# The product with gamma of four of five groups on GpSimd in the first experts' combining

## The chip, the cores and the metric

The kernel runs on one core of one Trainium2 chip. The metric is the device time of one execution in microseconds (us), lower being better. Several engines work side by side: TensorE (PE in the profile, its weight loads PEld), VectorE (DVE), ScalarE (ACT), GpSimd (POOL) and SyncE (SP, which issues transfers). Each engine runs its own instructions in order, and engines wait for one another through semaphores.

## The reference, cut to what matters

The program computes two rounds, each a graph stage followed by a mixture of experts. The change lies at the end of the first experts (16 experts, two for each row, rows of 256 values). For each of the 3125 rows:

```python
moe = jnp.sum(topk_w[..., None] * sel, axis=2)     # two weighted results of experts
y = x + moe                                        # here x is the normalised row, xn in the kernel
mu = jnp.mean(y, axis=-1, keepdims=True)
var = jnp.var(y, axis=-1, keepdims=True)
return (y - mu) / jnp.sqrt(var + EPS) * gamma + beta
...
x = x + _L0_ffn_ref(_layernorm(x, axis=-1)[None], ...)[0]
x = x + _L1_gnn_ref(_layernorm(x, axis=-1), ...)   # the next stage wants the normalised new x
```

## The kernel before

Rows lie on 128 partitions in 25 tiles of 256 values (`NT`); five tiles make a group (`J = 5`), so there are five groups (`NJ = 5`), and an operation on one group is 128 x 1280 values.

`feed_forward` runs the experts. Its last results are written by GpSimd to a buffer in memory (`put_rows`, line 2376), and then the class `Finish` combines them. SyncE reads both results of all rows back (`Finish.sync`, lines 2492 and 2495, into the tiles `f_hits` and `h`), and VectorE and ScalarE work through the five groups in turn. In the trace the rows being combined (`y`) are called `f_hits`, the running x is `parts_and_x`, and gamma is `f_gamma`.

On VectorE (`Finish.vector`) there are these steps for a group i:

- `sum_up(i)`: ten operations that add the two weighted results to xn (line 2553, five for each result), then the moments of the rows (lines 2538 to 2546: five collections of statistics and seven small operations).
- `scale_first(i)`: waits for ScalarE's square root of the variance (line 2509), then a reciprocal and a product of 128 x 5 (lines 2568 and 2569).
- `join(i)`: waits until ScalarE has normalised the group, multiplies by gamma (line 2560) and adds to x (line 2561). beta was added to x earlier.
- moments of the new x (lines 2538 to 2546 again, on `parts_and_x`).
- `scale_next(i)`: waits for the square root of that variance (line 2517), then five small operations (lines 2577 to 2584).

The steps of several groups are interleaved, and the order is written out by hand:

```python
for i in range(NJ):
    sum_up(i)
    if i:
        if i >= 2:
            scale_next(i - 2)
        join(i - 1)
    scale_first(i)
    if i:
        moments(c.x, 1, i - 1).then_inc(self.s_var2, 1)
scale_next(NJ - 2)
join(NJ - 1)
```

ScalarE (`Finish.scalar`) runs `normalise(0)`, and then `normalise(i)` and `next_rows(i - 1)` for each further group. `normalise(i)` is the square root of line 2509 and, after `scale_first(i)`, five operations that normalise the group's tiles (line 2513). `next_rows(i)` is the square root of line 2517 and, after `scale_next(i)`, five operations that make the rows for the next stage (line 2524). So the five operations of `next_rows(i - 2)` stand ahead of the square root of `normalise(i)` on ScalarE. SyncE stores each finished group (line 2499). GpSimd has nothing in this stretch after its last `put_rows`.

When the last group is stored, all engines meet, and the next stage starts: the aggregation over the edges, with its first operations in lines 701 to 809.

Of the kernel before, what the change touches and what calls it, by code (L numbers as in the profile page):

```python
# [7 lines left out]
ALU = mybir.AluOpType  # L8
# [11 lines left out]
P = 128  # L20
N, E, D = 3125, 103125, 256
# [4 lines left out]
J = 5  # L26
NJ = NT // J
# [63 lines left out]
class Steps:  # L91


    def __init__(self, engine, sem):
        self.engine, self.sem, self.base, self.n = engine, sem, 0, 0
# [85 lines left out]
def bc(ap, shape):  # L181
    return ap.to_broadcast(shape)
# [1781 lines left out]
def feed_forward(nc, c, I, name, ne, nf, tiles, softmax_first, logits, w1, b1, w2, b2, norm, act_fn, weight, slot, xn_table, ys, h_table, out):  # L1964
# [9 lines left out]
    with Core(nc) as k:  # L1974
# [61 lines left out]
        finish = None  # L2036
        if out is None:
            got = [hits_room[:, 0:NT * D].rearrange("p (t d) -> p t d", d=D), c.h[:, :, :]]
            finish = Finish(nc, c, k, name, I, ys, weight, got, b2s[:, :, :].rearrange("p e d -> p (e d)"), h_table)
        with nc.Block() as block:  # L2040
# [321 lines left out]
            @block.gpsimd  # L2362
            def _(pool):
                def add_rows(t):
                    pool.wait_ge(s_yb, t + 1)
                    if t:

                        pool.wait_ge(s_added[(t - 1) % Y], 16 * ((t - 1) // Y + 1))
                    pool.sem_inc(s_ask, 1)
                    pool.indirect_dma_start(ys, bass.IndirectOffsetOnAxis(ap=home[:, t:t + 1], axis=0), yb[:, t % Y, :], None, compute_op=ALU.add)\  # L2370
                        .then_inc(s_added[t % Y], 16)

                def put_rows(t):
                    pool.wait_ge(s_yb, t + 3)
                    pool.sem_inc(s_ask, 1)
                    pool.indirect_dma_start(ys, bass.IndirectOffsetOnAxis(ap=home[:, t:t + 1], axis=0), yb[:, t % Y, :], None).then_inc(s_added[t % Y], 16)

                Core.clear(pool)
                pool.wait_ge(s_token, 1)
                if out is not None:  # L2380
                    pool.wait_ge(s_home, 1)
                    pool.wait_ge(s_start, 32)
                else:
                    finish.clear_rest(pool)
                for t in range(tiles):
                    if t >= Q:

                        pool.wait_ge(s_xt, t - Q + 2)
                    pool.sem_inc(s_ask, 1)
                    pool.indirect_dma_start(xb[:, t % Q, :], None, xn_table,  # L2390
                                            bass.IndirectOffsetOnAxis(ap=token[:, t:t + 1], axis=0)).then_inc(s_x[t % Q], 16)
                    if out is not None and t >= Q:
                        add_rows(t - Q)
                    if out is None and t >= Q:
                        if t == Q:
                            pool.wait_ge(s_home, 1)
                        put_rows(t - Q)
                for t in range(tiles - Q, tiles):
                    if out is not None:
                        add_rows(t)  # L2400
                    else:
                        put_rows(t)


class RowNorm:
# [34 lines left out]
class Finish:  # L2440
# [3 lines left out]
    def __init__(self, nc, c, k, name, I, ys, weight, got, out_room, h_table):  # L2444
        self.nc, self.c, self.I, self.ys, self.weight, self.got, self.h_table = nc, c, I, ys, weight, got, h_table
        self.gamma, self.beta = k.sb(f"{name}_gamma", [P, D]), k.sb(f"{name}_beta", [P, D])
        self.out = out_room[:, 0:2 * J * W1].rearrange("p (q j d) -> p q j d", q=2, j=J)
        self.clip = k.sb(f"{name}_clip", [P, 2, NT])
        self.stats = k.sb(f"{name}_stats", [P, 2, J, 6])
        self.mean, self.gap, self.var, self.root = (k.sb(f"{name}_{x}", [P, 2, J]) for x in ("mean", "gap", "var", "root"))  # L2450
        self.rstd, self.down, self.rstd_src, self.down_src = (k.sb(f"{name}_{x}", [P, J]) for x in ("rstd", "down", "rstd_src", "down_src"))
        self.s_got = [k.sem(f"{name}_got{i}") for i in range(NJ)]
        self.s_saved = [k.sem(f"{name}_saved{q}") for q in range(2)]
        (self.s_gb, self.s_rest, self.s_clip, self.s_degrees, self.s_shift,  self.s_var1, self.s_root1, self.s_down1,
         self.s_even, self.s_var2, self.s_root2, self.s_down2, self.s_row, self.s_last) = (
            k.sem(f"{name}_n{x}") for x in ("gb", "rest", "clip", "degrees", "shift",  "var1", "root1", "down1",
                                            "even", "var2", "root2", "down2", "row", "last"))

    def tiles_of(self, i):
        return slice(i * J, i * J + J)  # L2460
# [5 lines left out]
    def clear_rest(self, pool):  # L2466
        for rows in self.got:
            pool.memset(rows[:, NT - 1, :], 0.0).then_inc(self.s_rest, 1)

    def degrees(self, act):  # L2470
        act.wait_ge(self.s_clip, 1)
# [61 lines left out]
    def vector(self, dve, v, st):  # L2533
        c, y, stats, mean, gap, var = self.c, self.got[0], self.stats, self.mean, self.gap, self.var

        def moments(rows, q, i):
            for j in range(J):
                last = v.bn_stats(stats[:, q, j, :], rows[:, i * J + j, :])
            st.link(last)
            v.tensor_tensor(mean[:, q, :], stats[:, q, :, 1], stats[:, q, :, 4], ALU.add)  # L2540
            v.tensor_tensor(gap[:, q, :], stats[:, q, :, 1], stats[:, q, :, 4], ALU.subtract)
            st.link(v.tensor_tensor(var[:, q, :], stats[:, q, :, 2], stats[:, q, :, 5], ALU.add))
            v.tensor_scalar_mul(mean[:, q, :], mean[:, q, :], -0.5)
            v.tensor_tensor(gap[:, q, :], gap[:, q, :], gap[:, q, :], ALU.mult)
            st.link(v.tensor_scalar(var[:, q, :], var[:, q, :], 1.0 / D, EPS, ALU.mult, ALU.add))
            return v.scalar_tensor_tensor(var[:, q, :], gap[:, q, :], 0.25, var[:, q, :], ALU.mult, ALU.add)

        def sum_up(i):
            dve.wait_ge(self.s_got[i], 32 if i < NJ - 1 else 64)
            for q in range(2):  # L2550
                for t in range(i * J, i * J + J):
                    to = c.xn[:, t, :] if q == 0 else y[:, t, :]
                    last = v.scalar_tensor_tensor(y[:, t, :], self.got[q][:, t, :], self.weight[:, q, t:t + 1], to, ALU.mult, ALU.add)
                st.link(last)
            moments(y, 0, i).then_inc(self.s_var1, 1)

        def join(i):
            ts = self.tiles_of(i)
            dve.wait_ge(self.s_even, (i + 1) * J)
            st.link(v.tensor_tensor(y[:, ts, :], y[:, ts, :], bc(self.gamma[:, :].unsqueeze(1), [P, J, D]), ALU.mult))  # L2560
            st.link(v.tensor_tensor(c.x[:, ts, :], c.x[:, ts, :], y[:, ts, :], ALU.add))

        def scale_first(i):
            dve.wait_ge(self.s_root1, i + 1)
            if i:

                dve.wait_ge(self.s_even, i * J)
            st.link(v.reciprocal(self.rstd[:, :], self.root[:, 0, :]))
            v.tensor_tensor(self.down[:, :], mean[:, 0, :], self.rstd[:, :], ALU.mult).then_inc(self.s_down1, 1)

        def scale_next(i):
            ts = self.tiles_of(i)
            dve.wait_ge(self.s_root2, i + 1)
            if i:

                dve.wait_ge(self.s_row, i * J)
            st.link(v.reciprocal(c.h_rstd[:, ts], self.root[:, 1, :]))
            st.link(v.tensor_tensor(c.h_down[:, ts], mean[:, 1, :], c.h_rstd[:, ts], ALU.mult))
            v.tensor_tensor(self.rstd_src[:, :], c.h_rstd[:, ts], c.norm_src[:, ts], ALU.mult)
            v.tensor_tensor(self.down_src[:, :], c.h_down[:, ts], c.norm_src[:, ts], ALU.mult).then_inc(self.s_down2, 1)  # L2580
            if i >= 2:

                dve.wait_ge(self.s_saved[i % 2], 16 * (i // 2))
            v.tensor_copy(self.out[:, i % 2, :, D], c.norm_src[:, ts]).then_inc(self.s_last, 1)

        dve.wait_ge(self.s_shift, NT)
        v.memset(self.out[:, :, :, D:W1], 0.0)
# [11 lines that stand above are left out]
        moments(c.x, 1, NJ - 1).then_inc(self.s_var2, 1)  # L2599
        scale_next(NJ - 1)  # L2600
# [241 lines left out]
```

## Time and profile before

| what | value |
|---|---|
| median of 3 runs | 3093.87 us (3089.11 to 3099.95) |
| the profiled execution, its own time | 3092.59 us |
| its span, from the first to the last instruction | 3091.0 us |
| TensorE busy | 2442.2 us (79%) |
| VectorE busy | 1786.1 us (58%) |
| GpSimd busy | 1742.3 us (56%) |
| ScalarE busy | 1450.7 us (47%) |

The span is the time between the first and the last instruction, and 1.6 us of the execution's own time lie around it. Shares of busy time are averages over stages that have different limits; the stretch that the change touches is about 80 us long, from 1361 to 1444 us after the span's start, and is read by itself.

### The profile page before, as it was taken

To read this page: it belongs to the slowest core of one execution; us is meant where nothing else is said; L and a number is where in the kernel's file an instruction comes from. 1 tells how busy PE (TensorE), PEld (TensorE's weight loads), DVE (VectorE), ACT (ScalarE), POOL (GpSimd) and SP (SyncE) were. 2 spreads that over 40 slices of the span, in tenths; PEclk is the share of its full clock that TensorE was granted. 3 is DMA by queue.
4 is the path that set the end of the run, shared out by engine and by line. 5 is a ranking of instruction groups with operands and counts; after the bars stand their busy time and mean duration, and the time that the engine had idled before them with its cause. 6 is when DMAs were issued, how large, how long until landed. Compare 5 with 4: busy or idle time off the path is not lost. (4 is left out here: it accounts for less than half of the span.)

```text
span 3091.0 us, 52879 instructions
## 1 busy us (share of the span) xinstructions
PE 2442.2 (79%) x14195; PEld 1910.2 (62%) x14195; DVE 1786.1 (58%) x5132; ACT 1450.7 (47%) x3766; POOL 1742.3 (56%) x1702
## 2 busy tenths in 40 slices
PE   1759999969999489850877777787877775899997
PEld 0336666747777478750655555555555554799996
DVE  7669889747788521037776666666666666311110
ACT  0357666535565333333644444444444433455553
POOL 1647777667774045422777777777777750233332
PEclk9989999989999589985998999988898987899998
DMA  6748777578886233543666666666666643443232
GB/s 226 253 143 233 227 209 211 168 227 257 263 251 186 85 109 103 168 128 125 197 186 185 180 186 184 182 182 187 181 187 185 190 119 101 121 106 77 49 65 64
DMA packets 289373, 516.56 MB, mean 167 GB/s; under 512 B 79344, under 2 KB 137057, under 8 KB 287084
## 3 DMA queue, kind: packets, MB, share of 16 engines
q0 software_dynamic: 86192, 225.20, 28.2%
q1 hardware_dynamic: 185532, 267.85, 26.4%
q10 hardware_dynamic: 17392, 20.46, 2.0%
q8 instruction: 116, 1.90, 0.2%
q14 instruction: 141, 1.16, 0.1%
HBM read 381.08 MB, written 137.11 MB: 168 GB/s over the span
## 5 line engine op out<-in xcount | busy, mean ns | idle before, releaser
L726 POOL DMA_INDIRECT agg_r_rows<-h_table,parts_and_x x832 | 831.0, 999 | 336.9 <-issue 230.1
L817 PE MATMUL agg_r_sums<-agg_r_rows,agg_r_onehot 128*128 128x257 f32 x1664 | 489.4, 422 | 259.9 <-DVE agg_r_rows L798 171.8
L817 PEld LDWEIGHTS agg_r_sums<-agg_r_rows,agg_r_onehot 128*128 128x128 f32 x1664 | 305.4, 203 | 396.3 <-issue 318.0
L686 ACT ACTIVATE agg_r_gap<-iota,parts_and_x 128x128 f32<-128x128 f32 x832 | 286.6, 392 | 449.8 <-PE agg_r_sums L817 419.8
L780 DVE TENSOR_TENSOR acc<-acc,agg_r_sums 128x257 f32 (+1 forms) x834 | 351.9, 422 | 129.1 <-PE agg_r_sums L817 44.9
L1723 POOL DMA_INDIRECT rl_buf<-r_table,kinds x304 | 327.6, 1078 | 150.0 <-issue 78.9
L2119 PEld LDWEIGHTS f_pH<-f_xT,f_w 128*128 128x128 f32 x2816 | 332.3, 195 | 40.0 <-ACT f_xT L2197 17.9
L2119 PE MATMUL f_pH<-f_xT,f_w 128*128 128x128 f32 x2816 | 346.7, 280 | 9.9 <-ACT f_xT L2197 4.5
L831 PE MATMUL agg_r_spread<-xn 128*128 128x257 bf16 x2664 | 350.2, 292 | 0.0
L1526 PE MATMUL la_acc<-la_parts,la_counts 128*128 128x512 f32 x1250 | 309.1, 404 | 29.3 <-DVE la_parts L1633 29.3
L2138 PE MATMUL f_pY<-f_w,f_hT 128*128 128x256 f32 x1408 | 325.6, 381 | 7.5 <-DMA f_w<-in_L_ffn_w 7.5
L831 PEld LDWEIGHTS agg_r_spread<-xn 128*128 128x128 bf16 x2664 | 279.6, 105 | 75.7 <-issue 10.0
L2206 ACT ACTIVATE f_hT<-f_pH,f_b 128x128 f32<-128x128 f32 x704 | 197.6, 372 | 263.9 <-PE f_pH L2119 263.6
L1723 POOL DMA_INDIRECT rm_buf<-r_table,kinds x250 | 245.1, 980 | 85.4 <-issue 66.8
L1526 PEld LDWEIGHTS la_acc<-la_parts,la_counts 128*128 128x128 f32 x1250 | 235.0, 190 | 89.9 <-issue 42.2
L2138 PEld LDWEIGHTS f_pY<-f_w,f_hT 128*128 128x128 f32 x1408 | 259.2, 191 | 39.3 <-DMA f_w<-in_L_ffn_w 8.6
L1433 DVE TENSOR_SCALAR b_oh<-b_numbers,b_code 128x400 bf16<-128x400 f16 x980 | 254.7, 324 | 0.0
L798 DVE TENSOR_TENSOR agg_r_rows<-agg_r_rows,agg_r_rel 128x514 f32<-128x514 f32 x305 | 211.0, 692 | 58.2 <-DMA agg_r_rows<-h_table,parts_and_x 56.9
L2370 POOL DMA_INDIRECT f_ys<-f_yb,f_home x56 | 88.2, 1575 | 272.8 <-DVE f_yb L2360 258.9
L1312 PE MATMUL b_strips<-b_oh,b_at 128*128 128x400 bf16 x980 | 199.1, 334 | 50.0 <-DVE b_oh L1433 44.5
L1566 ACT ACTIVATE la_counts<-matrix 128x640 fp32r<-128x640 fp8e4 x250 | 184.0, 737 | 112.8 <-PE la_acc L1526 85.8
L2354 DVE TENSOR_TENSOR f_plain<-f_pY,f_b 128x256 f32<-128x256 f32 x56 | 23.8, 425 | 361.8 <-PE f_pY L2138 361.8
(418 smaller groups left out, 3596.8 us busy)
## 6 DMA issues: line engine op xcount, KB each, us to landing
agg_r_rel<-relation_rows SPq DMA_DIRECT2D x305, 260.0 KB, 3.0
relation_rows<-rl_buf SPq DMA_DIRECT2D x152, 260.0 KB
relation_rows<-rm_buf SPq DMA_DIRECT2D x125, 260.0 KB, 3.3
agg_r_rows<-h_table,parts_and_x POOLq DMA_INDIRECT x832, 3.2
f_w<-in_L_ffn_W SPq DMA_DIRECT2D x18, 512.0 KB, 5.4
f_w<-in_L_ffn_W SPq DMA_DIRECT2D x9, 1024.0 KB, 4.8
f_w<-in_L_ffn_w SPq DMA_DIRECT2D x30, 256.0 KB, 3.1
f_w<-in_L_ffn_w SPq DMA_DIRECT2D x15, 512.0 KB, 3.6
```

Of the source, the lines that this page charges most:

```text
L686: last = nc.scalar.activation(gap[:, n % HOT, t, :], c.iota[:, 0:P], ACT.Abs, bias=c.tab["b_near"][:, column(g) + t:column(g) + t + 1])
L726: pool.indirect_dma_start(rows[:, n % SLOTS, t, :], None, table, bass.IndirectOffsetOnAxis(ap=indices[:, t:t + 1], axis=0)).then_inc(s_row ...
L780: v.tensor_tensor(here, here, sums[:, (2 * (n - LAG) + t) % BANKS, 0:used], ALU.add).then_inc(s_acc, 1)
L798: last = v.tensor_tensor(here, here, rel[:, n % SLOTS, :, 0:used], ALU.mult)
L817: last = nc.tensor.matmul(sums[:, (2 * n + t) % BANKS, 0:used], onehot[:, n % HOT, t, :], rows[:, n % SLOTS, t, 0:used], start=True, stop= ...
L831: last = nc.tensor.matmul(spread[:, t, 0:used], hot[:, r % 2, q, t * P:(t + 1) * P], parts[:, q, part, 0:used], start=q == 0 and part == 0 ...
L1312: last = nc.tensor.matmul(strips[:, n % BANKS, 0:CODES], at[:, n % 2, t, :], oh[:, n % 2, t, :], start=t == 0, stop=t == DEEP - 1)
L1433: last = v.tensor_scalar(oh[:, n % 2, t, :], numbers[:, :], code[:, q, 1, own, t:t + 1], None, ALU.is_equal)
L1526: last = nc.tensor.matmul(acc[:, n % 2, :], counts[:, i, j, :], parts[:, s, :], start=s == 0, stop=s == NT - 1)
L1723: pool.indirect_dma_start(self.buf[:, n, g, :], None, self.table, bass.IndirectOffsetOnAxis(ap=self.c.kinds[:, at:at + 1], axis=0)).then_i ...
L2119: last = nc.tensor.matmul(pH[s][:, f * P:(f + 1) * P], w1b[:, s, f // (FC // 2), at:at + P], xT[:, s, h, :], start=h == 0, stop=h == KD - 1)
L2138: last = nc.tensor.matmul(pY[s][:, 0:D], hT[:, s, f, :], w2b[:, s, f, :], start=f == 0, stop=f == FC - 1)
```

## The change

For the first four groups the product with gamma moves from VectorE to GpSimd. GpSimd makes the four products after its last `put_rows`, each as one instruction on 128 x 1280 values, and each waits until ScalarE has normalised the five tiles of the group (`s_even`). VectorE's addition of those groups waits for a new semaphore, `s_gamma`. The fifth group is as before.

```diff
@@ -2400,6 +2400,9 @@
                         add_rows(t)
                     else:
                         put_rows(t)
+                if finish:
+                    pool.wait_ge(finish.s_gb, 32)
+                    finish.products(pool)
...
@@ -2466,6 +2469,13 @@
...
+    def products(self, pool):
+        y = self.got[0]
+        for i in range(NJ - 1):
+            ts = self.tiles_of(i)
+            pool.wait_ge(self.s_even, (i + 1) * J)
+            self.nc.gpsimd.tensor_tensor(y[:, ts, :], y[:, ts, :], bc(self.gamma[:, :].unsqueeze(1), [P, J, D]), ALU.mult).then_inc(self.s_gamma, 1)
...
@@ -2556,8 +2566,11 @@
         def join(i):
             ts = self.tiles_of(i)
-            dve.wait_ge(self.s_even, (i + 1) * J)
-            st.link(v.tensor_tensor(y[:, ts, :], y[:, ts, :], bc(self.gamma[:, :].unsqueeze(1), [P, J, D]), ALU.mult))
+            if i < NJ - 1:
+                dve.wait_ge(self.s_gamma, i + 1)
+            else:
+                dve.wait_ge(self.s_even, (i + 1) * J)
+                st.link(v.tensor_tensor(y[:, ts, :], y[:, ts, :], bc(self.gamma[:, :].unsqueeze(1), [P, J, D]), ALU.mult))
             st.link(v.tensor_tensor(c.x[:, ts, :], c.x[:, ts, :], y[:, ts, :], ALU.add))
```

On GpSimd, at the end of the first experts and the start of the aggregation (`f_ys` is the experts' buffer, `agg_r_rows` the rows gathered for the aggregation, and `L136` clears semaphores):

```order
 L2376 DMA f_ys<-f_yb,f_home 14592x256 x5
+L2478 TENSOR_TENSOR f_hits<-f_hits,f_gamma 128x1280 x4
 L2040 UNCONDITIONAL_BRANCH
 L719 UNCONDITIONAL_BRANCH
 L726 DMA agg_r_rows<-h_table,parts_and_x 128x260 x24
-L136 ISA x48
+L136 ISA x49
```

Four products stand behind the last write of results and ahead of the end of the stage; one more semaphore is cleared among the aggregation's gathers.

On VectorE, at the combining of the second group, from the end of `scale_next(0)` over `join(1)` to `scale_first(2)`, in the kernel before:

```order
L2580 TENSOR_TENSOR f_down_src<-h_down,norm_src 128x5
L2584 COPY f_b<-norm_src 128x5
L2560 TENSOR_TENSOR f_hits<-f_hits,f_gamma 128x1280
L2561 TENSOR_TENSOR parts_and_x<-parts_and_x,f_hits 128x1280
L2568 RECIPROCAL f_rstd<-f_root 128x5
L2569 TENSOR_TENSOR f_down<-f_mean,f_rstd 128x5
```

The same place in the changed kernel:

```order
L2593 TENSOR_TENSOR f_down_src<-h_down,norm_src 128x5
L2597 COPY f_b<-norm_src 128x5
L2574 TENSOR_TENSOR parts_and_x<-parts_and_x,f_hits 128x1280
L2581 RECIPROCAL f_rstd<-f_root 128x5
L2582 TENSOR_TENSOR f_down<-f_mean,f_rstd 128x5
```

One large operation is gone between `scale_next` and `scale_first`, and the addition stands alone there; at the first, third and fourth group it is the same.

## Rows read from the trace of the kernel before

**Rows 1.** Busy us by stretch: length, PE, PEld, DVE, ACT, POOL, clock, DMA.

```profile
1370.00:1437.80 67.80, 0.00 (x0) 0.00 (x0) 64.62 (x215) 24.86 (x56) 0.00 (x0) 0.50 0.34 111
```

**Rows 2.** Timeline, GpSimd: start us, length us, operation, [idle before].

```profile
1445.59 0.99 POOL L726 DMA_INDIRECT agg_r_rows<-h_table,parts_and_x  x1 [83.57 <-PE agg_r_sums L809]
```

**Rows 3.** Timeline, end of the stretch: the last rows, the next stage's first work.

```profile
1437.68 2.56 ACT L2524 ACTIVATE f_b<-parts_and_x,f_down_src,f_rstd_src 128x256 f32<-128x256 f32 x5 [0.73 <-DVE f_down_src L2580]
...
1444.16 0.59 PE L809 MATMUL agg_r_sums<-zero_b 128*128 128x257 bf16 x2 [84.49 <-PEq L2040]
```

**Rows 4.** Timeline, VectorE and ScalarE at the first group's combining.

```profile
1376.93 0.21 ACT L2509 ACTIVATE f_root<-f_var 128x5 f32<-128x5 f32 x1 [19.43 <-DVE f_var L2546]
...
1377.17 0.19 DVE L2568 RECIPROCAL f_rstd<-f_root 128x5 f32<-128x5 f32 x1 [0.27 <-ACT f_root L2509]
...
1377.60 2.56 ACT L2513 ACTIVATE f_hits<-f_hits,f_down,f_rstd 128x256 f32<-128x256 f32 x5 [0.46 <-DVE f_down L2569]
...
1379.57 2.07 DVE L2553 SCALAR_TENSOR_TENSOR f_hits<-h,f_weight,f_hits 128x256 f32<-128x256 f32 x5
1381.68 1.73 DVE L2538 BATCH_NORM_STATS2 f_stats<-f_hits 128x6 f32<-128x256 f32 x5
1383.44 0.17 DVE L2540 TENSOR_TENSOR f_mean<-f_stats 128x5 f32<-128x5 f32 x1
...
1384.23 1.48 DVE L2560 TENSOR_TENSOR f_hits<-f_hits,f_gamma 128x1280 f32<-128x1280 f32 x1
1384.35 0.21 ACT L2509 ACTIVATE f_root<-f_var 128x5 f32<-128x5 f32 x1 [4.19 <-DVE f_var L2546]
1385.75 1.49 DVE L2561 TENSOR_TENSOR parts_and_x<-parts_and_x,f_hits 128x1280 f32<-128x1280 f32 x1
```

**Rows 5.** Timeline, VectorE and ScalarE at the second group's combining.

```profile
1387.70 2.56 ACT L2513 ACTIVATE f_hits<-f_hits,f_down,f_rstd 128x256 f32<-128x256 f32 x5 [3.14 <-DVE f_down L2569]
...
1390.13 2.06 DVE L2553 SCALAR_TENSOR_TENSOR f_hits<-f_hits,f_weight,xn 128x256 f32<-128x256 f32 x5
...
1397.53 1.48 DVE L2560 TENSOR_TENSOR f_hits<-f_hits,f_gamma 128x1280 f32<-128x1280 f32 x1
1397.58 2.57 ACT L2524 ACTIVATE f_b<-parts_and_x,f_down_src,f_rstd_src 128x256 f32<-128x256 f32 x5 [7.12 <-DVE f_down_src L2580]
1399.05 1.49 DVE L2561 TENSOR_TENSOR parts_and_x<-parts_and_x,f_hits 128x1280 f32<-128x1280 f32 x1
1400.05 0.19 ACT L2509 ACTIVATE f_root<-f_var 128x5 f32<-128x5 f32 x1
...
1400.57 0.19 DVE L2568 RECIPROCAL f_rstd<-f_root 128x5 f32<-128x5 f32 x1
```

**Rows 6.** GpSimd's groups by shape, first 5 us: busy us, mean ns | idle before.

```profile
L426 POOL IOTA matrix<- 128x808 int32 x1 | 0.8, 801 | 0.0
L420 POOL IOTA wide_i<- 128x512 int32 x1 | 0.6, 554 | 0.7 <-POOLq L201 0.7
L211 POOL TENSOR_SCALAR_AFFINE_SELECT ident<-ident 128x128 f32<-128x128 f32 x1 | 0.3, 282 | 0.0
...
L424 POOL TENSOR_SCALAR_AFFINE_SELECT alive<-alive 128x1 f32<-128x1 f32 x1 | 0.2, 186 | 0.1
```

**Rows 7.** Timeline, GpSimd issuing gathers beside trains of VectorE, two places.

```profile
84.76 7.88 DVE L1073 TENSOR_SCALAR parts_and_x<-parts_and_x,ln_mean,ln_var 128x256 f32<-128x256 f32 x24
...
85.72 6.83 POOL L1723 DMA_INDIRECT r_buf<-r_table,kinds  x1 [0.30 <-issue]
...
850.61 4.29 DVE L1633 TENSOR_TENSOR la_parts<-parts_and_x,la_parts 128x1280 fp32r<-128x1280 f32 x3
...
850.72 2.19 POOL L1723 DMA_INDIRECT rm_buf<-r_table,kinds  x1 [0.30 <-issue]
```

**Rows 8.** By source line, count, min/median/max ns: VectorE products, GpSimd gathers.

```profile
L1633 DVE TENSOR_TENSOR la_parts<-parts_and_x,la_parts x12: 418/1484/1493, 656.2 to 864.0; 128x1280 fp32r<-128x1280 f32 x8, 128x1024 fp32r<-128x1024 f32 x2, 128x256 fp32r<-128x256 f32 x2
...
L726 POOL DMA_INDIRECT agg_r_rows<-h_table,parts_and_x x832: 949/953/1662, 1445.6 to 2528.9; - x167
```

More of the change, by code:

```diff
@@ L2454, in __init__ @@
         (self.s_gb, self.s_rest, self.s_clip, self.s_degrees, self.s_shift,  self.s_var1, self.s_root1, self.s_down1,
-         self.s_even, self.s_var2, self.s_root2, self.s_down2, self.s_row, self.s_last) = (
+         self.s_even, self.s_var2, self.s_root2, self.s_down2, self.s_row, self.s_last, self.s_gamma) = (
             k.sem(f"{name}_n{x}") for x in ("gb", "rest", "clip", "degrees", "shift",  "var1", "root1", "down1",
-                                            "even", "var2", "root2", "down2", "row", "last"))
+                                            "even", "var2", "root2", "down2", "row", "last", "gamma"))
     def tiles_of(self, i):
```

## The prediction

> **What bounds the kernel now.** The change touches one stretch, the combining at the end of the first experts, so the shares over the whole span say little. I read the busy time by stretch first. From 1370.0 to 1437.8 us VectorE is busy for 64.62 of 67.80 us, ScalarE for 24.86, GpSimd and TensorE not at all [rows 1]. VectorE is the bound there. The timeline says the same: its operations stand end to end, and ScalarE mostly waits for it. The last rows are made at 1437.68, and the next stage's first matmul stands at 1444.16 with nothing beside this work [rows 3], so time taken from VectorE's chain should shorten the whole execution by as much, as long as nothing else is late next. GpSimd's next work in the trace is the gather at 1445.59, after 83.57 us of idle time [rows 2]; the products find it free, and no transfer of GpSimd's own stands behind them before the stage ends. The one more semaphore to clear, among the aggregation's gathers, I cost at nothing: gathers follow each other there without a gap that the clearing of the other 48 makes.
>
> **What is removed from VectorE.** A product with gamma takes 1.48 us, and the addition behind it starts 1385.75 - 1384.23 = 1.52 us after it [rows 4]. Four go: 6.08 us of VectorE's work. That is not yet time gained; what is late next has to be looked up at each place.
>
> First group. Without the product the addition stands at 1384.23 and ends at about 1385.7. Behind it is the reciprocal of `scale_first(1)`, which needs ScalarE's square root of 1384.35, done at 1384.56 [rows 4]. It is ready, so the whole 1.52 us is gained.
>
> Second group. The addition moves from 1399.05 to 1397.53 and ends at 1397.53 + 1.49 = 1399.02 [rows 5]. Behind it the reciprocal of `scale_first(2)` needs ScalarE's square root, and on ScalarE that stands behind the five operations of `next_rows(0)`, which VectorE itself released only at 1397.58 and which take 2.57 us. The root runs from 1400.05 to 1400.24 [rows 5]. Where VectorE has had to wait for a root, it went on 0.03 us after its end: 1376.93 + 0.21 against 1377.17 [rows 4]. So the reciprocal comes at 1400.27 instead of 1400.57 [rows 5]: of 1.52 us only 0.30 is gained, and 1.22 us becomes a wait for ScalarE. The third and fourth groups repeat this order. The fifth keeps its product.
>
> Sum of what can be gained: 1.52 + 3 x 0.30 = **2.42 us** of the 6.08.
>
> **What is added on GpSimd.** Each product waits for the end of ScalarE's five normalising operations: 1377.60 + 2.56 = 1380.16 for the first [rows 4], 1387.70 + 2.56 = 1390.26 for the second [rows 5]. The additions want them at 1384.23 and 1397.53. So there is a cover of 4.07 us for the first product and 7.27 us for the later ones. The queue behind a VectorE that waits for a product holds everything that follows: the addition, `scale_first`, and through it ScalarE.
>
> The trace of before has no product on GpSimd, so its price T is bounded. A generation of numbers costs (801 - 554) / (808 - 512) = 0.83 ns an element above some 0.13 us [rows 6]; 1280 elements in one such pass are 1.2 us, the lower end. Two reads and a write, each as a pass of its own, are 3 x 1.07 + 0.13 = 3.3 us, the upper end. The selection that reads 128 elements and writes 128 takes 282 ns against 186 ns for one, 0.76 ns an element [rows 6], so a read and its write go in one pass, and a second operand makes two: T = 2 x 1.07 + 0.13 = 2.3 us, which I take. All three lie under both covers, so VectorE would not wait for the products as such.
>
> In the Trainium skill, "GPSIMD Engine Reference" (section 3.1, Elementwise) has 4497 ns for an addition of two operands of 2048 elements; 1280 elements are then an estimated 2.8 us. No run here shows it yet, and it too lies under the covers.
>
> **What the two engines do to each other.** This decides the sign. The first product becomes ready at 1380.16, within VectorE's train of five operations at 1379.57, each with two inputs in the on-chip memory; behind it are 1.73 us of statistics with one input (from 1381.68), then small operations with two inputs (from 1383.44) [rows 4]. The second becomes ready at 1390.26, just after the train at 1390.13 has begun [rows 5]. Two places show GpSimd beside such trains. Beside 24 one-input operations an issue that takes 0.95 us otherwise [rows 8] took 6.83 us and ended as the train did; beside 128x1280 products with two inputs one took 2.19 us [rows 7], while those products kept to 1484 ns, at most 1493 [rows 8]. In both GpSimd waited and VectorE did not.
>
> So my forecast lets each product wait until the train ends and run from 1381.68 beside the statistics. It ends at 1381.68 + 2.3 = 1383.98, and the small operation of 1383.44 waits 0.54 us for it. With T = 1.2 that wait is zero, with 3.3 it is 1.57 us. Four times 0.54 is 2.16 us (0 to 6.3). Sum: -2.42 + 2.16 = **-0.26 us**, with ends at -2.4 and +3.9.
>
> The profiled execution took 3092.59 us, of which 3091.0 is span; the median of the runs is 3093.87. Against the profiled execution this gives 3092.3 us, against the median 3093.6, and that I forecast; ends 3091.5 and 3097.7.
>
> **Rivals.**
>
> Rival 1, GpSimd holds VectorE off (slower). A product that gets in between two operations of a train stops the train for its whole length. Each of the four costs T, in a part where ScalarE is not what VectorE waits for: 4T - 2.42, which is +2.4 us at 1.2, +6.8 at 2.3 and +10.8 at 3.3. It is slower than before from T = 0.61 us on. For it: the issue at 850.72 took 2.19 us, so it got going at about 852.0, as the first of the products ended and with the next directly behind it [rows 7]; GpSimd found its way in between. Against it: no operation of VectorE in these rows is longer for it, though an issue is not a reading product. Time: 3100.7 us.
>
> The Trainium skill's "SBUF — State Buffer" (section "Who interferes with whom") has this as a rule: a VectorE instruction with two inputs there and a GpSimd instruction that reads there exclude each other, and whichever is second waits until the first is done. Which one is first the page leaves to the order of issue. With the other page's estimate of 2.8 us the rival would cost +8.8 us.
>
> Rival 2, the two engines do not touch. Then all 2.42 us are gained: 3091.5 us. For it: VectorE's times beside issues are flat. Against it: GpSimd's are not [rows 7].
>
> Rival 3, the product is far dearer than its bounds. Above T = 4.07 the first addition waits; above 7.27 + 1.22 = 8.49 the later ones cost as well. At 12 us this is 12 - 4.07 - 1.52 + 3 x (12 - 8.49 - 0.30) = +16.0 us, 3109.9. Against it: no first use of an operation on GpSimd in the rows shows such a price [rows 6].
>
> That the change does nothing is no rival: the order on the engines shows four products on GpSimd and four fewer on VectorE.
>
> **How the numbers follow.** Forecast 0.40, rival 1 0.30, rival 2 0.23, rival 3 0.07. The measurement can tell about 0.3% from no change, 9.3 us here; the bounds are 3084.6 and 3103.2. No case goes below the lower one, since only 2.42 us are to be had: 0.03 for differences between runs. Above the upper one lies rival 1 with T over 2.93 us, about a third of it, and most of rival 3: 0.13. The rest, 0.84, is within. The range runs from 3089.5, which is rival 2 less 2 us for the spread of the median (the three runs span 10.8 us), to 3101.5, which takes in rival 1 up to T = 2.5 us. Outside lie the dearer part of rival 1, rival 3 and a little below, some 2 in 10.
>
> **What would show it.** On VectorE, reciprocals of `scale_first(2)` to `scale_first(4)` that wait about 1.2 us for ScalarE's root, and additions that start without a wait for GpSimd. On GpSimd, four products of 1.2 to 3.3 us that end after the train. If the forecast holds, the operations of the trains keep their 0.42 us and the small operation behind the statistics starts late. If rival 1 holds, one operation of a train has a gap or a length of about T. If rival 2 holds, neither. The stretch from 1370.05 to the last rows would be shorter by 0.3 us, longer by 7, or shorter by 2.4. A difference of more than 12 us from the median, or one that lies outside this stretch, would make the prediction wrong in its kind.

## The result, and the profile after

The changed kernel is slower. Over 20 runs of each, it took 3103.75 us (median; 3095.21 to 3112.26) against 3092.65 us (3086.37 to 3101.50). The ratio is 1.0032 with a 95% interval of 1.0022 to 1.0042, which is 9.9 us, between 6.8 and 13.0 (the medians lie 11.1 us apart). The forecast was 3093.6 us with a range up to 3101.5, so the time lies outside it, on the side of rival 1.

The profiled execution of the changed kernel took 3095.21 us with a span of 3093.6 us. It is the shortest of the 20, so the place of the loss is read from the combining stretch and not from the span. I measure that stretch on VectorE, from the start of the first weighted sum to the start of the last small copy of `scale_next(4)`. Before it is 1370.05 to 1437.57, which is 67.52 us; after it is 1363.91 to 1439.65, which is 75.74 us: **8.22 us longer**. That lies inside the interval of 6.8 to 13.0 us. The first and last operation, before and after:

```profile
1370.05 2.07 DVE L2553 SCALAR_TENSOR_TENSOR f_hits<-f_hits,f_weight,xn 128x256 f32<-128x256 f32 x5 [9.63 <-DMA h<-f_ys]
...
1437.57 0.17 DVE L2584 COPY f_b<-norm_src 128x5 f32<-128x5 f32 x1
```

```profile
1363.91 2.07 DVE L2563 SCALAR_TENSOR_TENSOR f_hits<-f_hits,f_weight,xn 128x256 f32<-128x256 f32 x5 [9.69 <-DMA h<-f_ys]
...
1439.65 0.17 DVE L2597 COPY f_b<-norm_src 128x5 f32<-128x5 f32 x1
...
1439.77 2.56 ACT L2534 ACTIVATE f_b<-parts_and_x,f_down_src,f_rstd_src 128x256 f32<-128x256 f32 x5 [0.73 <-DVE f_down_src L2593]
...
1446.29 0.59 PE L809 MATMUL agg_r_sums<-zero_b 128*128 128x257 bf16 x2 [92.81 <-PEq L2040]
```

From the start of the last rows to the next stage's first matmul it is 1446.29 - 1439.77 = 6.52 us, against 6.48 before [rows 3], so nothing is lost at the border to the next stage.

The busy times of this stretch, the columns as in [rows 1]:

```profile
1363.90:1439.70 75.80, 0.00 (x0) 0.00 (x0) 69.02 (x211) 24.75 (x55) 11.87 (x4) 0.50 0.30 99
```

VectorE has four instructions fewer and is busy for longer (69.02 us against 64.62), and GpSimd is busy for 11.87 us with four products, 2.97 us each. ScalarE is unchanged (the window of before only reaches a little way into its last five operations). An engine that does less work and is busy longer is being held up inside its instructions. VectorE's idle time in these windows grows as well, from 3.18 to 6.78 us; that comes from the wait shown for the second group below, which occurs three times. The timeline at the first group, which answers to [rows 4], shows where:

```profile
1373.44 4.69 DVE L2563 SCALAR_TENSOR_TENSOR f_hits<-h,f_weight,f_hits 128x256 f32<-128x256 f32 x5
1374.18 2.88 POOL L2478 TENSOR_TENSOR f_hits<-f_hits,f_gamma 128x1280 f32<-128x1280 f32 x1 [18.36 <-ACT f_hits L2523]
1378.16 1.73 DVE L2548 BATCH_NORM_STATS2 f_stats<-f_hits 128x6 f32<-128x256 f32 x5
1379.93 0.17 DVE L2550 TENSOR_TENSOR f_mean<-f_stats 128x5 f32<-128x5 f32 x1
...
1380.72 1.48 DVE L2574 TENSOR_TENSOR parts_and_x<-parts_and_x,f_hits 128x1280 f32<-128x1280 f32 x1
```

The train of five operations takes 4.69 us instead of 2.07. The product starts inside it and takes 2.88 us; the statistics and the small operations behind it are as they were. The addition at 1380.72 follows the small operations without a wait, 3.7 us after the product's end, so it is not the new semaphore that costs. By source line (count, min/median/max ns), the two trains before, then the two after, and the one operation by itself in a narrow window:

```profile
L2553 DVE SCALAR_TENSOR_TENSOR f_hits<-f_hits,f_weight,xn x25: 478/480/485, 1370.0 to 1418.3; 128x256 f32<-128x256 f32 x25
L2553 DVE SCALAR_TENSOR_TENSOR f_hits<-h,f_weight,f_hits x25: 476/480/485, 1372.2 to 1420.4; 128x256 f32<-128x256 f32 x25
```

```profile
L2563 DVE SCALAR_TENSOR_TENSOR f_hits<-f_hits,f_weight,xn x25: 470/477/3103, 1363.9 to 1420.7; 128x256 f32<-128x256 f32 x25
L2563 DVE SCALAR_TENSOR_TENSOR f_hits<-h,f_weight,f_hits x25: 472/480/3104, 1366.0 to 1422.7; 128x256 f32<-128x256 f32 x25
```

```profile
1374.23 3.10 DVE L2563 SCALAR_TENSOR_TENSOR f_hits<-h,f_weight,f_hits 128x256 f32<-128x256 f32 x1
```

The medians are those of before (480 ns; operations of a train start 0.40 us apart and overlap, so that five take 2.07 us), the longest are 3.10 us. Each of the four products meets one train, and in it exactly one operation is long: it starts 0.05 us (first group) to 0.18 us after the product does and ends 0.28 us after the product's end. That is one operation held for the length of one product.

The second group, which answers to [rows 5]:

```profile
1385.09 4.68 DVE L2563 SCALAR_TENSOR_TENSOR f_hits<-f_hits,f_weight,xn 128x256 f32<-128x256 f32 x5
...
1385.31 3.00 POOL L2478 TENSOR_TENSOR f_hits<-f_hits,f_gamma 128x1280 f32<-128x1280 f32 x1 [8.25 <-ACT f_hits L2523]
1389.81 2.07 DVE L2563 SCALAR_TENSOR_TENSOR f_hits<-h,f_weight,f_hits 128x256 f32<-128x256 f32 x5
...
1395.12 1.49 DVE L2574 TENSOR_TENSOR parts_and_x<-parts_and_x,f_hits 128x1280 f32<-128x1280 f32 x1
1395.17 2.56 ACT L2534 ACTIVATE f_b<-parts_and_x,f_down_src,f_rstd_src 128x256 f32<-128x256 f32 x5 [9.75 <-DVE f_down_src L2593]
1397.64 0.19 ACT L2519 ACTIVATE f_root<-f_var 128x5 f32<-128x5 f32 x1
...
1397.92 0.19 DVE L2581 RECIPROCAL f_rstd<-f_root 128x5 f32<-128x5 f32 x1 [1.31 <-issue]
```

Here the first train of the next sum is hit, the second is untouched. And the reciprocal of `scale_first(2)` now waits 1.31 us. The profile names no releaser for it, but it starts 0.09 us after the end of ScalarE's root (1397.64 + 0.19). The prediction had this wait, with 0.03 us after the root.

### The profile page after: what moved, and what is told of

It reads as the page before. It is cut to its first block and busy times, and to the rows that moved or that the text cites. A ratio compares the mean times of both kernels' runs of the same rounds, so it can differ in the third digit from the quotient of the medians.

```text
span 3093.6 us, 52881 instructions
## 1 busy us (share of the span) xinstructions
PE 2442.4 (79%) x14195; PEld 1909.0 (62%) x14195; DVE 1789.9 (58%) x5128; ACT 1450.6 (47%) x3766; POOL 1760.7 (57%) x1706
## 5 line engine op out<-in xcount | busy, mean ns | idle before, releaser
L1723 POOL DMA_INDIRECT rm_buf<-r_table,kinds x250 | 244.2, 977 | 85.4 <-issue 70.8
```

The costliest lines, as they stand in the source:

```text
L1723: pool.indirect_dma_start(self.buf[:, n, g, :], None, self.table, bass.IndirectOffsetOnAxis(ap=self.c.kinds[:, at:at + 1], axis=0)).then_i ...
```

## The experiments

Two theories for the held operations. Theory 1: a GpSimd instruction that reads the on-chip memory holds off a VectorE instruction with two inputs there, for its whole length. Theory 2: any work of GpSimd slows VectorE. A third question was whether the rest of the loss comes from elsewhere. All runs at a glance, with the stretch as defined above, the aggregation behind it from its first sum to its last, and the time of the execution that was profiled. Each experiment's stretch comes from one profile:

| run | stretch, us | aggregation, us | execution, us |
|---|---|---|---|
| kernel before, three profiles | 67.52, 67.51, 67.49 | 1090.7, 1095.4, 1096.4 | 3092.59, 3091.01, 3093.56 |
| changed kernel, three profiles | 75.74, 75.73, 75.74 | 1093.2, 1101.1, 1092.7 | 3095.21, 3109.64, 3103.42 |
| products behind the train | 69.60 | 1095.5 | 3097.96 |
| spare product | 78.03 | 1096.3 | 3113.25 |
| spare copy | 71.46 | 1100.3 | 3105.04 |
| spare zeroing | 67.48 | 1092.5 | 3094.73 |
| five small products | 73.24 | 1098.8 | 3102.56 |
| root first | 72.44 | 1095.4 | 3103.99 |
| products behind the train, root first | 66.22 | 1097.1 | 3097.17 |
| three tiles on GpSimd | 64.33 | 1104.4 | 3101.03 |

**Products behind the train.** The product waits in addition for the last operation of VectorE's second train.

```diff
             pool.wait_ge(self.s_even, (i + 1) * J)
+            pool.wait_ge(self.s_link, self.train_end[i + 1])
...
```

Further lines, not shown, note on VectorE where each train ends.

> The changed kernel, but each product on GpSimd also waits until VectorE's train of ten two-input operations (sum_up of the next group) has ended. The combining stretch, from VectorE's first weighted sum to its last small copy, is 67.5 us in the kernel before and 75.7 us in the changed one. Theory 1 (a GpSimd instruction that reads on-chip memory holds off VectorE instructions with two inputs there, for its whole length, and no others): the trains take 2.07 us again, the statistics keep 1.73 us beside the product, and the first small two-input operation behind them waits about 1.4 us; stretch 67.5 - 2.3 + 4 x 1.4 = 70.8 us. Theory 2 (any work on GpSimd slows VectorE): the statistics grow by about 2.6 us as the trains did; stretch 75.7 us.

The timeline:

```profile
1377.10 2.07 DVE L2565 SCALAR_TENSOR_TENSOR f_hits<-h,f_weight,f_hits 128x256 f32<-128x256 f32 x5
1379.20 1.73 DVE L2550 BATCH_NORM_STATS2 f_stats<-f_hits 128x6 f32<-128x256 f32 x5
1379.35 2.88 POOL L2479 TENSOR_TENSOR f_hits<-f_hits,f_gamma 128x1280 f32<-128x1280 f32 x1 [19.82 <-DVE f_hits L2565]
1380.97 1.29 DVE L2552 TENSOR_TENSOR f_mean<-f_stats 128x5 f32<-128x5 f32 x1
1382.18 0.15 DVE L2553 TENSOR_TENSOR f_gap<-f_stats 128x5 f32<-128x5 f32 x1
```

The train is back at 2.07 us. The statistics, one input each, run beside the product in their 1.73 us. The first small operation with two inputs takes 1.29 us instead of 0.17 and ends as the product does. This is what my forecast drew, made by force, and it still makes the stretch 2.1 us longer than before: four waits of 1.1 us against 2.2 us gained. (The 70.8 us that I had expected came of waits of 1.4 us.) Theory 2 is out for the statistics, the only VectorE instructions with one input that ran beside a product here.

**Spare work on GpSimd.** Three kernels keep all products on VectorE and only let GpSimd do something at the same four moments, into a place that nobody reads: a product, a copy, or zeros.

```diff
+            pool.wait_ge(self.s_even, (i + 1) * J)
+            if i:
+                pool.wait_ge(self.s_spare, i)
+            self.nc.gpsimd.tensor_tensor(self.spare, self.got[1][:, ts, :], bc(self.gamma[:, :].unsqueeze(1), [P, J, D]), ALU.mult).then_inc(self.s_spare, 1)
...
```

The others have `tensor_copy(self.spare, self.got[1][:, ts, :])` and `memset(self.spare, 0.0)` in its place.

> The kernel before, with all of its products on VectorE, and beside them four products of 128x1280 on GpSimd at the moments of the changed kernel, read from finished rows and written to a spare place that nobody reads or waits for. Theory 1: one operation of each train is held by 2.6 us; stretch 67.5 + 4 x 2.62 = 78.0 us. Were the loss of the changed kernel a wait for the product's result instead, nothing would wait here: 67.5 us.

> As the spare product, but GpSimd copies 128x1280 values (one input read, one output written). Theory 1: the copy reads on-chip memory, so it holds VectorE's two-input operation for its own length, some 1.2 to 1.5 us: one operation of each train 0.8 to 1.2 us longer, stretch 70.7 to 72.3 us. If only instructions of GpSimd with two inputs hold VectorE off: 67.5 us.

> As the spare product, but GpSimd sets 128x1280 values to zero (nothing read). Theory 1: no operation of VectorE is longer than in the kernel before; stretch 67.5 us. Theory 2: one operation of each train is longer by about the length of the instruction, some 1 us; stretch 71 us.

The first group's operation meets VectorE's second train (`h,f_weight,f_hits`), the other three meet its first (`f_hits,f_weight,xn`). By source line, both trains beside the product:

```profile
L2567 DVE SCALAR_TENSOR_TENSOR f_hits<-f_hits,f_weight,xn x25: 472/477/3124, 1371.6 to 1430.4; 128x256 f32<-128x256 f32 x25
L2567 DVE SCALAR_TENSOR_TENSOR f_hits<-h,f_weight,f_hits x25: 471/479/3127, 1373.7 to 1432.5; 128x256 f32<-128x256 f32 x25
```

Beside the copy, and the copy itself:

```profile
L2567 DVE SCALAR_TENSOR_TENSOR f_hits<-f_hits,f_weight,xn x25: 471/479/1471, 1368.2 to 1420.4; 128x256 f32<-128x256 f32 x25
L2567 DVE SCALAR_TENSOR_TENSOR f_hits<-h,f_weight,f_hits x25: 471/479/1476, 1370.3 to 1422.5; 128x256 f32<-128x256 f32 x25
...
L2482 POOL COPY f_b<-h x4: 1248/1390/1393, 1378.5 to 1418.1; 128x1280 f32<-128x1280 f32 x4
```

Beside the zeros, and the zeroing itself:

```profile
L2567 DVE SCALAR_TENSOR_TENSOR f_hits<-f_hits,f_weight,xn x25: 473/479/486, 1368.9 to 1417.1; 128x256 f32<-128x256 f32 x25
L2567 DVE SCALAR_TENSOR_TENSOR f_hits<-h,f_weight,f_hits x25: 478/479/486, 1371.0 to 1419.2; 128x256 f32<-128x256 f32 x25
...
L2482 POOL MEMSET f_b<- x4: 1165/1166/1166, 1379.1 to 1415.7; 128x1280 f32 x4
```

The spare product costs 10.5 us of the stretch although nothing waits for it: the whole loss is contact between the engines. (It is the 8.2 us of the changed kernel and the 2.2 us that the changed kernel gains by four products fewer.) The copy, 1.25 to 1.39 us long and with one input, holds one operation of each train to 1.47 us; it costs 3.9 us. The zeros, 1.17 us long in the same place, hold nothing: 486 ns at most, and the stretch is the one of before. So it is GpSimd's reading that matters on its side, and theory 1 stands for what was tried: trains and small operations with two inputs are held, the statistics are not. A product beside other VectorE operations with one input was not run. The rule on the exclusion that the prediction cited from the Trainium skill ("SBUF — State Buffer", section "Who interferes with whom") agrees with these three runs and with the one before them.

**Five small products.** Each product in five of one tile.

```diff
-            self.nc.gpsimd.tensor_tensor(y[:, ts, :], y[:, ts, :], bc(self.gamma[:, :].unsqueeze(1), [P, J, D]), ALU.mult).then_inc(self.s_gamma, 1)
+            for t in range(i * J, i * J + J):
+                last = self.nc.gpsimd.tensor_tensor(y[:, t, :], y[:, t, :], self.gamma[:, :], ALU.mult)
+            last.then_inc(self.s_gamma, 1)
```

> The changed kernel, with each product of 128x1280 on GpSimd cut into five of 128x256. If the engines take turns, each in the order in which it asks, every small product holds one operation of the train for its own length of about 0.7 us, and the five together cost as much as the one: stretch 74.8 to 78.8 us. If an operation of VectorE that stands ready always goes ahead of GpSimd, the small products find no room in a train and run beside the statistics: stretch about 69 us, with trains of 2.07 us.

```profile
1387.47 3.93 DVE L2565 SCALAR_TENSOR_TENSOR f_hits<-f_hits,f_weight,xn 128x256 f32<-128x256 f32 x5
...
1387.69 4.29 POOL L2479 TENSOR_TENSOR f_hits<-f_hits,f_gamma 128x256 f32<-128x256 f32 x5 [5.91 <-ACT f_hits L2525]
```

By source line, the products and the first train:

```profile
L2479 POOL TENSOR_TENSOR f_hits<-f_hits,f_gamma x20: 719/900/904, 1377.8 to 1421.6; 128x256 f32<-128x256 f32 x20
```

```profile
L2565 DVE SCALAR_TENSOR_TENSOR f_hits<-f_hits,f_weight,xn x25: 474/483/947, 1367.5 to 1421.0; 128x256 f32<-128x256 f32 x25
```

The engines take turns: the five products run through the train, about 0.90 us each, and the operations of VectorE between them take 0.94 us instead of 0.48. The second expectation is out, VectorE has no precedence. The sum was lower than I had put it (73.2 against 74.8 to 78.8 us): an operation that is held in the train loses 0.46 us and not 0.7. In the train the products start 0.86 us apart, which is less than the 0.72 us of a product beside the statistics and the 0.40 us from one operation of a train to the next together, so part of the two goes on at the same time.

**Root first.** ScalarE's square root for group i is put ahead of the five operations that make the rows of group i - 2.

```diff
+        for i in range(NJ):
+            root(i)
+            if i >= 2:
+                next_rows(i - 2)
+            normalise(i)
+            if i:
+                next_root(i - 1)
...
```

> The changed kernel, with ScalarE's square root for group i put ahead of the five operations that make the rows of group i - 2. Theory: the reciprocals of the third to fifth group start 0.03 us after the addition instead of 1.3 us after it, and the stretch falls from 75.7 by 3 x 1.27 to 71.9 us, while the held operations of the trains keep their 3.1 us. If something else than ScalarE's order delays these reciprocals, the stretch stays at 75.7 us.

```profile
1400.95 0.21 ACT L2519 ACTIVATE f_root<-f_var 128x5 f32<-128x5 f32 x1 [9.17 <-DVE f_var L2565]
...
1401.47 1.48 DVE L2583 TENSOR_TENSOR parts_and_x<-parts_and_x,f_hits 128x1280 f32<-128x1280 f32 x1
...
1402.99 0.19 DVE L2590 RECIPROCAL f_rstd<-f_root 128x5 f32<-128x5 f32 x1
...
1435.54 0.19 DVE L2599 RECIPROCAL h_rstd<-f_root 128x5 f32<-128x5 f32 x1 [0.75 <-ACT f_root L2529]
```

The reciprocal follows the addition at 0.04 us. The stretch falls by 3.30 of the expected 3.8 us; the other half microsecond is a new wait at the end, where the root for `scale_next(3)` now stands behind more work of ScalarE and VectorE waits 0.75 us for it instead of 0.27.

**Both, and a version that uses it.** With both changes the four products on GpSimd shorten the stretch, to 66.22 us. That is half a microsecond more than expected, by the same new wait at the end as with the root first (0.74 us). And since the statistics offer about 1.65 us without contact, three of five tiles on GpSimd just about fit in them.

> Both together: products behind VectorE's trains, and ScalarE's root first. The four removed products give their full 6.08 us, the small operation behind the statistics waits 1.08 us four times as in the run with the products behind the trains: stretch 67.5 - 6.1 + 4.3 = 65.7 us, 1.8 us below the kernel before.

> A version made from these runs: GpSimd multiplies three of the five tiles of a group (128x768) behind the train, VectorE the other two (128x512), and ScalarE's root comes first. A product of 768 is estimated at 1.8 us from the 2.89 us of 1280, about as long as the 1.65 us from its start to the first small operation with two inputs, so that operation waits 0.1 to 0.2 us. VectorE's product shrinks from 1.48 to about 0.7 us. Stretch 67.5 - 4 x 0.8 + 4 x 0.15 = 64.9 us, 2.6 us below the kernel before; over the whole run this is 0.08%, at the edge of what five rounds can tell.

```profile
1389.82 1.73 DVE L2560 BATCH_NORM_STATS2 f_stats<-f_hits 128x6 f32<-128x256 f32 x5
1389.93 1.81 POOL L2480 TENSOR_TENSOR f_hits<-f_hits,f_gamma 128x768 f32<-128x768 f32 x1 [10.05 <-DVE f_hits L2575]
1391.59 0.18 DVE L2562 TENSOR_TENSOR f_mean<-f_stats 128x5 f32<-128x5 f32 x1
```

The small operation takes 0.18 us: nothing is held. The stretch is 64.33 us, 3.2 us below the kernel before. Over the whole execution this can't be seen: the median of 11 runs is 3094.45 us against 3095.53 in 14 runs of the kernel before, and the ratio is 1.000 with an interval of 0.999 to 1.0009. I don't call it faster.

**Both kernels again.** The stretch gives 8.2 us, and the middle of the measured difference is 9.9. To see whether something outside the stretch adds to it, both kernels were run and profiled twice more, on another chip than the experiments.

> The kernel before, unchanged, looked at again, to see how far the aggregation behind the stretch scatters by itself: it took 1090.7 us from its first to its last sum in the first profile, and 1092.5 to 1104.4 in the profiles of the changed kernel and the experiments. If that is scatter, it lies anywhere from 1090 to 1104 here; if the changed kernels' aggregation is longer for a reason of their own, it lies at 1091 to 1092 again. The combining stretch is 67.5 us either way.

> The changed kernel, unchanged, looked at again. Stretch 75.7 us. Scatter: aggregation anywhere from 1090 to 1104 us. A reason of its own: 1093 us or more, above both looks at the kernel before.

> As the first look again at the kernel before: stretch 67.5 us; aggregation 1090 to 1104 us if it scatters, 1091 to 1092 us if not.

> As the first look again at the changed kernel: stretch 75.7 us; aggregation 1090 to 1104 us if it scatters, above the kernel before if not.

The stretch repeats to 0.03 us. The aggregation scatters by 6 us in the kernel before (1090.7 to 1096.4) and by 8 us in the changed one (1092.7 to 1101.1), and the two overlap. So the 8.2 us are firm, and a further microsecond or two can't be told from scatter with three profiles of each; they lie within the interval. The lowest of the changed kernel (1092.7) is below two of the three of the kernel before, so nothing here shows a longer aggregation, but whether it adds anything stays open.

## Why the prediction was wrong

- **What bounds the stretch, and where it ends up:** right. VectorE's chain sets its length, and the loss sits in it.
- **What is removed:** right. The first group gains its 1.52 us (to the reciprocal it is 1382.24 - 1380.72 = 1.52 us from the addition's start, and was 1387.28 - 1384.23 = 3.05 us from the product's). At the second the addition's start to the reciprocal takes 1397.92 - 1395.12 = 2.80 us, where the product's start to the reciprocal took 3.04 us [rows 5]: 0.24 us gained against a forecast of 0.30, since the reciprocal came 0.09 us after the root and not 0.03. The run with the root first shows that ScalarE's order is the reason for the rest.
- **The price of the product:** mis-sized. Taken was 2.3 us of 1.2 to 3.3; it is 2.88 us beside the statistics, and also in the first group, where it starts 0.05 us ahead of the train's next operation; in the other groups, where it starts 0.18 us ahead of it, it is 3.00. Zeros of the same shape take 1.17 us and a copy 1.25, so one pass was well put (1.2 us), but the second operand costs more than another pass. The estimate of 2.8 us from the Trainium skill's "GPSIMD Engine Reference" (section 3.1, Elementwise), which the prediction gave beside its own, was nearer. This size alone would have turned the sign: with 2.88 us each small operation waits 1381.68 + 2.88 - 1383.44 = 1.12 us, and the forecast's own sum gives 4 x 1.12 - 2.42 = +2.1 us. The run with the products behind the train, which is that arrangement, measured +2.1. That is not the loss of the changed kernel, though; for that the next step had to be wrong too.
- **What the two engines do to each other: this step failed.** I let the product wait for the end of VectorE's train, from two rows in which an issue of GpSimd waited beside a train and VectorE did not [rows 7, 8]. The rows were also read too far: the issue at 850.72 ended at 850.72 + 2.19 = 852.91, and its train, the only one of the two with two inputs, at 850.61 + 4.29 = 854.90 [rows 7]. So it did not wait for the train's end; only the issue beside the operations with one input did. And an issue is not a product: zeros of GpSimd, which read nothing, held no operation of VectorE, so that VectorE was not longer beside an issue says nothing of an instruction that reads (whether an issue reads anything there, no run shows). The product gets in behind the operation in progress and holds the next one, 2.62 us each time. That was rival 1, at 0.30, and what it had read from the issue at 850.72, that GpSimd finds its way in between, came true for the products.
- **The sum by rival 1:** it gave 4T - 2.42, with T for the time that the train stands still. With the measured hold of 3.10 - 0.48 = 2.62 us an operation, 4 x 2.62 - 1.52 - 3 x 0.24 = 8.24 us, against 8.22 in the stretch. The hold is a little less than the product's length. At the T of 2.3 us that I had taken it was +6.8, and the range that I drew ended at T = 2.5. Had it gone to the upper bound of the price that I had worked out myself, 3.3 us, it would have held the time.
- **Rivals 2 and 3:** out. The engines do touch, and no addition waited for a product.

## What to carry to other kernels

An idle GpSimd does not make work moved from VectorE free: what counts is what VectorE does at that moment. Beside the statistics, with one input each, a product cost nothing. Beside a train of instructions with two inputs it stopped the train for nearly its whole length, here 2.6 us for a product that saved 1.5. One input is no general pass: beside 24 operations with one input an issue of GpSimd waited until they had ended [rows 7], and a product beside such operations was not tried. Before moving a piece, look at what VectorE does in the moments in which the piece would run, and gate it to moments that a run has shown to be free; and follow what is late next, since on three of four places ScalarE's order ate most of the gain.

## What the runs showed of the hardware that I had not expected

- A GpSimd copy with one input holds VectorE's two-input operation as well (1.47 us instead of 0.48, for a copy of 1.25 to 1.39 us), while zeros of 1.17 us hold nothing.
- A train of VectorE without a gap is no protection: GpSimd goes in behind the operation that is running, and with several short products the two engines alternate one by one, 0.94 and 0.90 us each.
- The contact reaches tiny operations: one of 128 x 5 values, with two inputs, took 1.29 us instead of 0.17 and ended 0.02 us after the product. One with one input did not stand in that place in any run.
- GpSimd's product of two operands took 0.72 us for 256 elements a partition, 1.81 us for 768 and 2.88 us for 1280, which is 2.1 ns for each further element.
